# A whole two-layer model in one kernel: six unread TensorE products per row, another place for the last router's scratch, and another order of the first loads

## The reference, cut to what matters

```
x = x + mamba2(layernorm(x))        # 32 heads of 64, state 128, causal conv of 4 taps, gate, rms norm
x = x + ffn(layernorm(x))           # weights quantized to -1, 0, 1:
                                    #   gamma = mean(abs(w)); clip(round(w / gamma), -1, 1)
                                    #   w3 @ (sigmoid(w1 @ x) * (w2 @ x)), 704 hidden
x = x + attention(layernorm(x))     # 16 heads of 16, alibi, causal
x = x + moe(layernorm(x))           # 64 experts, 6 of them per token, 64 slots each, plus a shared expert
```

## Time and profile before

| | |
|---|---|
| median of 3 runs | 1318.38 us (1317.02 to 1319.73) |
| profiled execution, its own time | 1316.61 us |
| span of the profile, first to last instruction | 1314.8 us |
| mean granted clock of PE | 0.958 of full speed |
| busy: PE, DVE, ACT, POOL | 1118.4, 884.8, 656.9, 555.9 us |
| start, up to the first scan of row 0 | 63.0 us |
| rows 0, 1, 2, from first scan to first scan | 282.1, 282.4, 283.4 us |
| moved by DMA | 159.56 MB |

### The profile page before, as it was taken

One profiled execution on the slowest core, in us unless ns is written; L12 is line 12 of the kernel. 1 busy time (PEld: TensorE's weight loads), 2 busy tenths in 40 slices (PEclk: granted clock), 3 DMA queues, 4 the chain that ended last, 5 costly groups with the idle time before them and its releaser, 6 DMA issues.

```text
span 1314.8 us, 24377 instructions
## 1 busy us (share of the span) xinstructions
PE 1118.4 (85%) x8378; PEld 722.3 (55%) x8380; DVE 884.8 (67%) x1850; ACT 656.9 (50%) x1575; POOL 555.9 (42%) x725
## 2 busy tenths in 40 slices
PE   2799998898999988989999988989999879877940
PEld 2355566665555556655555566655555556653520
DVE  4477886565878875657877875657777766662427
ACT  3655524666555525657554335666555245621630
POOL 0255661220387751210777821201777712143760
PEclk9899999899999999999999998999999999988975
DMA  8366553300253314101433323002433544077888
GB/s 325 105 213 190 183 176 77 97 2 21 91 161 114 113 47 108 50 4 35 145 124 117 104 77 94 5 22 65 144 110 114 187 109 145 2 257 239 159 199 323
DMA packets 120137, 159.56 MB, mean 121 GB/s; under 512 B 11632, under 2 KB 82928, under 8 KB 119280
## 3 DMA queue, kind: packets, MB, share of 16 engines
q1 hardware_dynamic: 106384, 131.73, 32.5%
q0 software_dynamic: 9216, 19.98, 5.8%
q10 hardware_dynamic: 4416, 6.29, 1.3%
HBM read 104.55 MB, written 40.83 MB: 111 GB/s over the span
## 4 chain that ended last, share of the span: by engine, by line
PE 47%; DVE 19%; ACT 12%; issue 9%; POOL 7%; DMA 4%; SPq 0%; POOLq 0%; DVEq 0%; ACTq 0%
PE bank L1187 10%; DVE pool_c L1690 6%; PE bank L1229 5%; PE bank L1110 4%; ACT joint L851 3%; PE bank L1410 3%; PE bank L1367 3%; PE bank L1395 3%; PE bank L1332 2%; ACT pool_c L812 2%; POOL joint L2200 2%; PE bank L1223 2%; PE bank L1497 2%; PE bank L1208 2%; PE bank L1216 2%
## 5 line engine op out<-in xcount | busy, mean ns | idle before, releaser
L1187 PE MATMUL bank<-xm,joint 128*128 128x512 f32 x544 | 269.1, 619 | 18.6 <-DVE pool_c L1690 12.9
L2200 POOL TENSOR_TENSOR joint<-joint 128x512 f32<-128x512 f32 x128 | 163.9, 1282 | 208.2 <-DVE joint L1706 205.1
L1690 DVE SCALAR_TENSOR_TENSOR pool_c<-bank,params,pool_c 128x511 f32<-128x511 f32 (+2 forms) x216 | 161.4, 748 | 95.9 <-ACT pool_c L812 90.0
L1187 PEld LDWEIGHTS bank<-xm,joint 128*128 128x128 f32 x544 | 98.5, 195 | 122.1 <-issue 92.2
L1891 DVE TENSOR_REDUCE nmax<-bank 128x1 f32<-128x384 f32 (+3 forms) x176 | 109.6, 637 | 60.6 <-PE bank L1368 59.8
L1229 PE MATMUL bank<-wout,pool_c 128*128 128x256 f32 x512 | 121.8, 381 | 3.4 <-DVE pool_c L1731 3.4
L851 ACT ACTIVATE joint<-bank,dt_ 128x64 f32<-128x64 f32 x512 | 111.7, 342 | 22.4 <-PE bank L1110 22.2
L1229 PEld LDWEIGHTS bank<-wout,pool_c 128*128 128x128 f32 x512 | 95.7, 190 | 36.1 <-issue 21.7
L2194 POOL DMA_INDIRECT xslot<-xrow,slots x96 | 96.0, 1000 | 26.7 <-issue 22.0
L821 ACT ACTIVATE pool_c<-pool_c 128x512 f32<-128x512 f32 x64 | 40.3, 630 | 116.4 <-DVE pool_c L1690 116.4
L977 ACT ACTIVATE pool_c<-bank 128x512 f32<-128x512 f32 (+1 forms) x156 | 83.2, 551 | 18.0 <-PE bank L1397 15.6
(11 more groups left out here) (272 smaller groups left out, 2361.6 us busy)
## 6 DMA issues: line engine op xcount, KB each, us to landing
pool_b<-dA_rows SPq DMA_DIRECT2D x64, 256.0 KB, 3.4
pool_b<-dec_rows SPq DMA_DIRECT2D x96, 128.0 KB, 3.6
joint<-pool_b SPq DMA_DIRECT2D x96, 128.0 KB, 2.4
acc<-xrow SPq DMA_DIRECT2D x13, 640.0 KB, 6.2
joint<-dA_rows SPq DMA_DIRECT2D x32, 256.0 KB
dA_late<-dA_rows SPq DMA_DIRECT2D x32, 256.0 KB
joint<-acc SPq DMA_DIRECT2D x32, 256.0 KB, 6.8
xslot<-xrow SPq DMA_DIRECT2D x16, 321.0 KB, 5.1
```

The costliest lines, as they stand in the source:

```text
L1187: last = mm(bank[:, :], win[:, k, col:col + P], xm[:, k, :], start=(k == 0), stop=(k == KD - 1))
L1690: ins = v.scalar_tensor_tensor(out=cv[:, n:L], in0=bank[:, 0:L - n], scalar=convw[:, ci, TAPS - 1 - n:TAPS - n], in1=cv[:, n:L], op0=ALU.m ...
L2200: M_ready.inc(p.tensor_tensor(M[u % 2][:, hs_, :], Lx[:, hs_, :], cbm[:, c * P:(c + 1) * P].unsqueeze(1).to_broadcast([P, 4, P]), ALU.mult))
```

## The change

It joins several edits:

- `stay_awake` is called at six more places: four products in `ffn` behind `mean_squares(1)`, two ahead of its third tile, four ahead of the first query products, three (eight in the last row) and three on either side of `norm_T(2, 1)` in `second_queries`, five in `between` ahead of `norm_T(3, 1)` of the row that is done, and nine in the last row's `finish` ahead of its `norm_T(3, 1)`. That is 63 products in rows 0 to 2 and 30 in row 3. The 58 products of the end become 72.
- The last router's scratch has its own place (`last_rt`), and `xm`, `mixed` and `pob` for its tables. So `wout` is free earlier: four pairs of experts go there with group `in_row`, the group `in_slots` is gone, and `in_values` has one pair less.
- At the start the half of `win` that holds x, B, C and the step sizes is loaded ahead of the FFN weights, the gates' half behind them. `step_products` waits for that half alone. Absolute values, thresholds and the quantization move into `between(None, 0)`, and `project_in` of the first tile goes ahead of `step_sums`. Waits for the quantized weights stand ahead of the first use of their places.

```diff
@@ routers, places of the expert weights
-        routers.append(Router(wout_[:, 0:2048], wout_[:, 2048:2816], wout_[:, 2816:3328], pob[:, :, :].rearrange("p t n -> p (t n)")))
+        last_rt = sb("last_rt", [P, 1736])
+        routers.append(Router(last_rt, xm[:, :, :].rearrange("p k n -> p (k n)")[:, 0:768], mixed[:, 1024:1536],
+                              pob[:, :, :].rearrange("p t n -> p (t n)")))
...
-        in_row = places(ffnw, 0, W1 + W2) + places(flat(xnT), 0) + places(flat(xn), 0) + places(mixed, 0)
-        in_scores, in_values = places(pool_a, *range(0, 8192, W1 + W2)), places(pool_c, *range(0, 8192, W1 + W2))
-        in_slots = places(wout_, 0, 1024, 2048)
+        in_row = places(ffnw, 0, W1 + W2) + places(flat(xnT), 0) + places(flat(xn), 0) + places(mixed, 0) + places(wout_, 0, 1024, 2048, 3072)
+        in_scores, in_values = places(pool_a, *range(0, 8192, W1 + W2)), places(pool_c, *range(0, 7168, W1 + W2))
@@ SP
+            w_in_loaded[0].inc(sp.dma_start(win[:, :, INTER:PROJ], a["win"][:, :, INTER:PROJ]))
             for dst, src in ffn_loads:
                 w_ffn_loaded.inc(sp.dma_start(dst, src))
-            for lo, hi in ((INTER, PROJ), (0, INTER)):
-                w_in_loaded[lo == 0].inc(sp.dma_start(win[:, :, lo:hi], a["win"][:, :, lo:hi]))
+            w_in_loaded[1].inc(sp.dma_start(win[:, :, 0:INTER], a["win"][:, :, 0:INTER]))
...
             load_weights(2)
-            sp.wait_ge(slots_ready.sem, slots_ready.upto(2, b))
-            load_weights(3)
@@ ACT
+            def magnitude(i):
+                act.wait_ge(w_ffn_loaded.sem, 16 * len(ffn_loads))
+                act.wait_ge(pro_act.sem, 1 + i)
+                pro_act.inc(sa.activation(magnitudes, wf[i], ACT.Abs, accum_out=absum[:, i:i + 1]))
@@ ACT, between
                 m(tap, tile_b)
+                if done is None:
+                    step_decays()
+                    magnitude(0)
                 m(read_rows)
...
                 m(silu, tile_c)
+                if done is None:
+                    magnitude(1)
+                    magnitude(2)
                 r(router_scores)
                 m(tap, ("x", 0, 1))
@@ PE, ffn
                 mean_squares(1)
+                stay_awake(4, pb[5])
                 pe.wait_ge(ln_done.sem, ln_done.upto(pair_count(b, 1, 0)))
                 at(h_lo_done, 1)
                 for n in range(2 * FT + 2):
                     p_, f = divmod(n, FT)
+                    if n == 2:
+                        stay_awake(2, pb[5])
...
                         norm_T(2, 0)
+                    if n == FT + 5:
+                        stay_awake(4, pb[5])
@@ PE, second_queries
+                stay_awake(3 if coming is not None else 8, pb[2])
                 norm_T(2, 1)
+                stay_awake(3, pb[2])
                 queries_keys(1, 0)
@@ PE, finish
                 positions(None, 0)
+                stay_awake(9, pb[5])
                 norm_T(3, 1)
...
-                stay_awake(58, pb[3])
+                stay_awake(72, pb[3])
@@ PE, between
                 m(project_in, tile_b)
+                if done is None:
+                    step_sums()
...
                 r(router_logits, 0, logit_bank(0, None))
+                r(stay_awake, 5, pb[1])
                 r(norm_T, 3, 1)
                 r(router_logits, 1, logit_bank(0, None))
                 m(project_in, ("x", 0, 1))
+                if done is None:
+                    weight_means()
@@ DVE, between
                 r(best_groups)
+                if done is None:
+                    thresholds()
+                    ternary(0)
                 m(convolve, ("x", 0, 2))
+                if done is None:
+                    ternary(1)
+                    ternary(2)
```

More of the change, by code:

```diff
@@ L613, in build @@
                       for e in range(2)]
-        wf = [carve(pool_a, i * 1536, 1536) for i in range(3)]
+        wf = [carve(pool_a, 2048, 1536), carve(pool_b, 2048, 1536), carve(pool_a, 5120, 1536)]
         masks = carve(pool_a, 4608, 2 * P)
-        low = [carve(pool_a, 4864 + i * 768, 768, F16) for i in range(3)]
+        low = carve(pool_b, 6144, 768, F16)
+        magnitudes = carve(pool_a, 0, 1536)
         wt = [w.rearrange("p k n -> p (k n)") for w in (w1q[:, :, :], w2q[:, :, :], w3q[:, :, :])]
@@ L870, in mixer_steps @@
             def mixer_steps():
+                if b == 0:
+                    act.wait_ge(pro_dve.sem, PRO_DVE)
                 for s in range(LAST + 1):
@@ L1059, in _ @@
                 norm_copy(0, p_)
-            act.wait_ge(w_ffn_loaded.sem, 16 * len(ffn_loads))
-            for i in range(3):
-                last = sa.activation(pool_b[:, i * 1536:(i + 1) * 1536], wf[i], ACT.Abs, accum_out=absum[:, i:i + 1])
-            pro_act.inc(last)
-            act.wait_ge(pro_dve.sem, PRO_DVE)
+            act.wait_ge(pro_dve.sem, 2)
             step_logs()
-            step_decays()
             between(None, 0)
@@ L1140, in step_products, with weight_means @@
                 dt_mm.inc(last)
+            def weight_means():
+                pe.wait_ge(pro_act.sem, 4)
+                pro_pe.inc(mm(pb[5][:, 0:3], ones[:, :], absum, start=True, stop=True))
             def step_sums():
@@ L1569, in _ @@
                 norm_T(0, p_)
-            pe.wait_ge(pro_act.sem, 2)
-            pro_pe.inc(mm(pb[7][:, 0:3], ones[:, :], absum, start=True, stop=True))
             normed(0)
-            for s in w_in_loaded:
-                pe.wait_ge(s.sem, 16)
+            pe.wait_ge(w_in_loaded[0].sem, 16)
             step_products()
-            step_sums()
             between(None, 0)
@@ L2035, in finish, with thresholds, ternary @@
                 add_shared()
+            def thresholds():
+                dve.wait_ge(w_ffn_loaded.sem, 16 * len(ffn_loads))
+                v.tensor_copy(maskb[:, :], masks[:, 0:P])
+                v.tensor_copy(maskTb[:, :], masks[:, P:2 * P])
+                dve.wait_ge(pro_pe.sem, 1)
+                link(v.tensor_scalar(thr, pb[5][:, 0:3], 1.0 / (FF * D), 1e-8, ALU.mult, ALU.add))
+                link(v.tensor_scalar(nthr, thr, -0.5, None, ALU.mult))
+                link(v.tensor_scalar(thr, thr, 0.5, None, ALU.mult))
+            def ternary(i):
+                link(v.tensor_scalar(low, wf[i], nthr[:, i:i + 1], None, ALU.is_lt))
+                last = v.scalar_tensor_tensor(out=wt[i], in0=wf[i], scalar=thr[:, i:i + 1], in1=low, op0=ALU.is_gt, op1=ALU.subtract)
+                if i < 2:
+                    link(last)
+                else:
+                    pro_dve.inc(last)
             def between(done, coming):
@@ L2209, in mixer_steps @@
             def mixer_steps(done, coming):
+                if coming == 1:
+                    pool.wait_ge(pro_dve.sem, PRO_DVE)
                 at(dec_ready, 3)
```

31 lines of the change are left out of this document (8 added, 23 removed).

## The result

| | kernel before | changed kernel |
|---|---|---|
| median | 1317.97 us (1317.02 to 1319.73, 4 runs) | 1297.76 us (1296.81 to 1299.52, 4 runs) |
| ratio | | 0.9842, 95% interval 0.9828 to 0.9856 |
| profiled execution, its own time | 1316.61 us | 1299.52 us |
| span of the profile | 1314.8 us | 1297.7 us |
| mean granted clock of PE | 0.958 | 0.969 |

The account below looks back on a forecast made before the run. No engine was taken to bound the kernel throughout; waits between engines count, PE holding 47% of the chain. Start -9.8, rows -9.4 and end -5.8 sum to -25.0, giving 1293.4 us, range 1286 to 1304.

Parts of the forecast that it names:

- Start: Up to row 0's first scan: loading the needed half of `win` first saves 9.8 us, bounds -6.2 and -11.9.
- the cover of the quantization: In the start's convolutions, DVE's 8.16 us of quantization fits into waits for ACT's tap and costs nothing; uncovered, 8.2.
- from there the stage goes on in its old order: In the start, after the tap of (x, 0, 1), the stage continues as before, keeping the 9.8 us gained.
- Rows: Unread products in the rows keep PE at full clock: query products 6.5 us, `between` 3.0, less 0.1; -9.4 in all.
- clock isn't held: Rival, chance 0.18: the rows' few unread products don't hold PE's clock, the rows term goes, 1302.8 us.
- End: Last router to program end: logits -1.0, last scatter's landing -2.85, expert products -2.0; -5.8 us, bounds -1 and -6.3.
- The third term: At the end, first expert products and transposes at full clock through 14 more unread products: 2.0 us, bounds 0 and -2.4.
- what the first output gains is gained at the end: POOL's adds follow the first expert product's output and pace the rest, so its gain of 2.0 us reaches the end.
- signs of being wrong: Step size products waiting past 14; query products of 3.78; DVE `ffnw` waits; last unread product ending behind the tokens' landing.
- Scatters stay slow: Rival, chance 0.12: late scatters still share DMA engines with remaining weights, the 2.85 us isn't gained, 1296.3 us.
- Preparation on the path: Rival, chance 0.06: at the start ACT's 4.5 and DVE's 8.2 us don't fit in waits; start +1.6, time 1304.8 us.
- The slower case: Rival, chance 0.02: unread products run at half clock and exceed their waits in rows and end, +23, 1341 us.

Follow-up runs that it names:

- the third trace: Third profile of the unaltered changed kernel, run beside three kernels with further unread products; 1299.06 us, ratio 0.9844 against the kernel before.
- The start alone: Kernel before with only the new order of first loads, absolute values and quantization, no added unread products; 1310.86 us, ratio 0.9930.
- the rows' products alone: Kernel before with only the unread products of ffn, second_queries and between added, start and end unchanged; 1309.79 us, ratio 0.9922.
- after_again: The unaltered changed kernel measured once more for a second profile; 1295.77 us, ratio 0.9821 against the kernel before.

## Why the prediction held, and where it was off

**The sign, the range and the likeliest case** were right: all three parts gain by themselves, and none of the rivals took over. It was 4.8 us too far down in the first measurement, 1.3 in the second (-23.7) and 3.7 in the third (-21.3).

**Start (-9.8; measured -7.9, -7.9, -9.8).** The working was right up to the first tap within 0.1 us (two errors of 0.35 cancel there), and so was the cover of the quantization. Mis-sized were the way from there to the tap of (x, 0, 1), 13.86 instead of 12.83 us in the first trace, and the step "from there the stage goes on in its old order": both kept PE's durations as they were. By stage times that is 0 to 1.9 us; that the third trace has -9.8 to the tenth is luck. Unread products in this stage's pauses bring the scan to 50.6 to 51.1, which shows that PE's clock is what the stage loses.

**Rows (-9.4).** For the query products in row 0 to 2 and the tile products of `between` I had 7.6; the traces show 6.5, 5.7 and 7.1. Taking the second queries' groups away loses 4 to 9 us, so the mechanism is shown. The step that failed is row 3's: I counted -2.8 there with the logits, and did not ask which pauses come between. The three profiles show -0.65, -3.0 and -0.6. The last projection is slow in all of them; in the second one the scores behind the transposes of norm 3 and the logits are at full clock, and row 3 gives what was forecast, while in the other two these are slow too. The start alone makes that projection slow too (3.78), without a single added product, and the rows' products alone do as well (3.56), so neither is needed for it. The rival "clock isn't held" was not decided once for all rows, as I had put it, but place by place and in part from execution to execution. FFN's ten products neither cost nor gain, as forecast.

**End (-5.8).** The landing gave -3.1 for -2.85, and in the kernel with that edit alone -2.6; the logits gave up to -0.9 for -1.0. The third term, -2.0 for expert products at full clock, had its mechanism right and its condition not assured. In the first trace the add comes only 0.3 us earlier relative to the landing, since two of the three groups were still slow; in `after_again`, with all at full clock, it comes 1.7 earlier. The step that did not hold is "what the first output gains is gained at the end": from the first add to the end it takes 103.5 to 104.3 us in the changed kernel's three traces and 102.9 before. Over all traces this stretch goes from 102.3 to 105.1; POOL's adds wait now and then for DVE's targets, for ACT's scaled products or for an earlier add to land (1.62, 2.14 and up to 3.02 us in the first trace). What sets that stays open, and no experiment was made on it.

One of the signs of being wrong did show: in `after_again` PE goes from the last unread product to the tokens' transposes without a wait, so the tokens were there first. Of the three profiles this is still the one in which the add comes soonest behind the landing (10.5).

**Rivals.** Scatters stay slow: refuted. Preparation on the path: refuted for DVE, with 2.05 us of cover left, and 0.25 when PE is faster; ACT's share was in the sum. The slower case: the products ran at full clock in nearly all places (0.81 for three), and where they were slow (1.49) they cost below a microsecond.

## What to carry to other kernels

When a change removes a slow stretch of the matrix engine, don't book the gain at the end of the program: follow the engine's next pauses, since a shift of some microseconds alone can make another stretch slow. Read such gains from several profiles, and let the ones that differ without a change of code set the smallest effect that a single trace can show (here 1 to 3.5 us in a stage). Put filler products into the pauses that a consumer waits behind, ahead of the fall, and leave out those whose removal costs nothing.

## What was not expected of the hardware

The same pauses, with the same busy time ahead of them (2.09 and 2.10 us of 4 at row 3's last projection), went with a fall of PE's clock to half in one kernel and with none in the other. What decides between the two stays open. Within one program it differs from execution to execution: the query product of row 2 took 1.99, 2.77 and 1.99, and the tile records at 23.2 us 5.30, 5.30 and 3.60.

The first tile takes 3.76 us for four records, twice the 1.88 of the first tile at 293.74 in the same trace, while the granted clock reads 1.00 in that window:

```profile
14.00:18.00 4.00, 4.00 (x14) 2.98 (x14) 0.58 (x2) 0.88 (x2) 0.00 (x0) 1.00 1.03 423
```

Traffic doesn't explain it. In the kernel before, the first tile takes 3.37 us at 31.83, and there the column reads 1.00 while the DMA engines move nothing:

```profile
31.80:35.00 3.20, 3.20 (x6) 1.22 (x5) 0.00 (x0) 0.45 (x2) 3.12 (x2) 1.00 0.00 0
```

So ahead of the first recorded fall the durations tell PE's level and the clock column doesn't.
